# A router's top six experts marked by match-replace: the ranks' transposes and the search of each chunk move to earlier places

## What is computed

```python
logits = x @ gate_w.T
scores = jax.nn.softmax(logits, axis=-1)
topk_w, topk_i = jax.lax.top_k(scores, K)          # K = 6 of E = 64
...
pos = ...   # place of the token among those of its expert, in order of tokens
valid = pos < CAP                                  # CAP = 64
buf = zeros((E, CAP + 1, H)).at[flat_i, slot].set(x[token_ids])
```

```python
proj = hidden_states @ in_proj_w.T;  x, gate = split(proj)
xc = silu(causal_conv(x, 4 taps) + conv_b)
ts, B, C = split(xc @ x_proj_w.T)
```

## Time and profile before

| | us |
|---|---|
| median of 3 runs | 1360.59 (1357.25 to 1361.22) |
| the profiled execution | 1356.37 |
| its span in the trace | 1354.4 |
| stage 1 in it | 264.0 |
| VectorE busy in the span | 1094.3 (81%) |
| TensorE busy in the span | 1277.3 (94%) |
| granted TensorE clock, mean | 0.986 |

### The profile page before, as it was taken

The page is one execution under the profiler, slowest core; times in us unless marked ns, Lnnn a source line. Parts: engine busy times, 40 slices in busy tenths (PEclk is TensorE's granted clock), DMA queues, the critical chain, the costliest instruction groups (busy, mean ns, idle before and its releaser), DMA issues.

```text
span 1354.4 us, 53446 instructions
## 1 busy us (share of the span) xinstructions
PE 1277.3 (94%) x21591; PEld 802.9 (59%) x21591; DVE 1094.3 (81%) x1260; ACT 902.9 (67%) x1920; POOL 878.0 (65%) x522
## 2 busy tenths in 40 slices
PE   6898989599999999999999999999999899999998
PEld 5666767345555545555545555545555578787876
DVE  5798989779999979999889999889999464655554
ACT  4755666478798878888878888778787253434343
POOL 3445348268998978989979899889998330303030
PEclk9999999889999999999999999999999899999999
DMA  8252544859999999999999999999898753122130
GB/s 290 96 229 105 215 153 161 263 166 287 281 308 284 288 273 265 299 298 265 307 260 281 298 265 314 298 262 303 263 309 277 250 201 119 68 80 107 51 134 31
DMA packets 129758, 304.82 MB, mean 225 GB/s; under 512 B 18560, under 2 KB 20352, under 8 KB 127872
## 3 DMA queue, kind: packets, MB, share of 16 engines
q1 hardware_dynamic: 122096, 285.13, 64.3%
q0 software_dynamic: 7600, 18.91, 7.0%
HBM read 213.91 MB, written 56.77 MB: 200 GB/s over the span
## 4 chain that ended last, share of the span: by engine, by line
PE 53%; DVE 10%; issue 9%; POOL 3%; ACT 3%; DMA 1%; DVEq 1%; ACTq 0%; POOLq 0%
PE p_dBx L1337 14%; PE p_dBx L1396 7%; PE p_y L1346 7%; DVE state L1026 7%; PE p_g L1323 6%; PE p_g L1306 4%; PE p_y L1407 2%; PE p_g L1407 2%; PE p_u L1407 2%; PE p_dt L1407 2%; PE p_dt L1286 2%; POOL h_times_C L961 2%; PE p_u L1292 1%; PE p_u L1306 1%; ACT dA L1176 1%
## 5 line engine op out<-in xcount | busy, mean ns | idle before, releaser
L1026 DVE TENSOR_TENSOR_SCAN state<-dA,state_carry,p_dBx 128x512 f32<-128x512 f32 x512 | 626.1, 1266 | 77.0 <-PE p_dBx L1337 74.7
L961 POOL TENSOR_TENSOR h_times_C<-state,C_bcast 128x1024 f32<-128x1024 f32 x128 | 318.0, 2485 | 56.8 <-DVE state L1026 55.9
L961 POOL TENSOR_TENSOR C_bcast<-state,C_bcast 128x1024 f32<-128x1024 f32 x128 | 319.4, 2770 | 23.3 <-DVE state L1026 22.2
L1337 PEld LDWEIGHTS p_dBx<-B_diagonals,step_rows 64*32 64x32 f32 x16384 | 237.1, 106 | 150.4 <-issue 147.6
L1337 PE MATMUL p_dBx<-B_diagonals,step_rows 64*32 64x128 f32 x16384 | 311.2, 276 | 12.6 <-DVE state L1026 7.1
L1176 ACT ACTIVATE dA<-dt_blocks_even,A_par 128x512 f32<-128x512 f32 x256 | 169.6, 710 | 21.5 <-DMA dt_blocks_even<-step_rows 21.5
L1176 ACT ACTIVATE dA<-dt_blocks_odd,A_par 128x512 f32<-128x512 f32 x256 | 169.6, 710 | 20.5 <-DMA dt_blocks_odd<-step_rows 20.5
L280 POOL TENSOR_TENSOR w_in_parts_lo<-C_bcast,w_in_parts_hi 128x512 fp32r<-128x512 f32 x64 | 90.2, 1411 | 107.1 <-ACT w_in_parts_hi L493 106.8
L976 POOL TENSOR_TENSOR step_rows<-step_rows 128x512 f32<-128x512 f32 x16 | 21.9, 1402 | 182.0 <-DMA step_rows<-moe 182.0
L371 DVE SCALAR_TENSOR_TENSOR conv_out<-conv_in,conv_w,conv_out 128x512 f32<-128x512 f32 x96 | 96.1, 1010 | 8.7 <-ACT conv_out L515 6.4
L1306 PE MATMUL p_u<-w_up_pair,step_rows 128*64 128x352 f32 x512 | 92.0, 478 | 3.7 <-issue 2.7
(11 more groups left out here) (186 smaller groups left out, 2114.0 us busy)
## 6 DMA issues: line engine op xcount, KB each, us to landing
w_gate_pair<-in_w_gate SPq DMA_DIRECT2D x32, 1408.0 KB
w_up_pair<-in_w_up SPq DMA_DIRECT2D x32, 1408.0 KB, 7.9
w_down_pair<-in_w_down SPq DMA_DIRECT2D x66, 512.0 KB
dt_blocks_odd<-step_rows SPq DMA_DIRECT2D x256, 64.0 KB
dt_blocks_even<-step_rows SPq DMA_DIRECT2D x240, 64.0 KB
w_down_pair<-in_w_down SPq DMA_DIRECT2D x33, 384.0 KB
g_d<-y_gated SPq DMA_DIRECT2D x33, 256.0 KB, 4.8
sz_d<-silu_gate SPq DMA_DIRECT2D x32, 256.0 KB, 2.1
```

The lines of the kernel that those rows point to most:

```text
L961: pool.tensor_tensor(hc[m][:, b, :, :], hb[:, q, :, :], Cb[:, NM * cp + GS * m:NM * cp + GS * m + GS, :], ALU.mult).then_inc(s_hc, 1)
L1026: ins = dve.tensor_tensor_scan(hb[:, g % NBUF, s, :], dA[:, g % NBUF, s, :], pB[:, g % 2, :].rearrange("p (t s) -> p s t", s=GS)[:, s, :], ...
L1337: ins = pe.matmul(out[DB * p:DB * p + DB, half, j, :, :], dtxT[k, j * P + DB * b:j * P + DB * b + DB], diag[k, ND * cp + 2 * j + p // 2, a ...
```

## The change

`max_index`, the cast, the six comparisons, their sum and the constant `expert_iota` go. In `scores` the last two of the eight largest are overwritten by -1, `match_replace` writes a copy of the scores in which the six largest are -2, and one instruction makes `(copy < 0) * rank`. The ranks' transposes stand in front of tile 8 in every chunk (`RANKS_TURN`; before in front of tile 12 in the last chunk and behind tile 15 in the others), `take_V` behind the first tap of conv 5, and every chunk's search in parts: one behind conv 5, two behind conv 6, one behind conv 7. SP no longer waits for the ranks before it loads the up weights into the place that the comparisons used.

```diff
-        RSTD_AT, RANKS_TURN, X_TURN, SEARCHES, PER_CHUNK = 12, 12, 12, CAP // 16, (T // P) // (NCH - 1)
+        RSTD_AT, RANKS_TURN, X_TURN, SEARCHES, PER_CHUNK = 12, 8, 12, CAP // 16, (T // P) // (NCH - 1)
...
                 if c == NCH - 1:
-                    sp.wait_ge(s_val, NCH)
                     sp.wait_ge(s_spread, 16 * NB * NB)
...
-            pool.iota(eioi[:, :, :], [[0, TJ], [1, E]], base=0, channel_multiplier=0).then_inc(s_const, 1)
...
                 settled()
+                chain(dve.memset(m8[:, :, TOPK:], -1.0))
+                settled()
                 for j in range(TJ):
-                    chain(dve.max_index(ix[:, j, :], m8[:, j, :], xs[:, j, H:XS]))
+                    chain(dve.match_replace(marked[:, j, :], m8[:, j, :], xs[:, j, H:XS], -2.0))
                 settled()
-                chain(dve.tensor_copy(ixf[:, :, :], ix[:, :, :]))
-
-            def ranks(c):
-
-                settled()
-                for k in range(TOPK):
-                    chain(dve.tensor_tensor(eq[:, k, :].rearrange("p (j e) -> p j e", j=TJ), eio[:, :, :],
-                                            ixf[:, :, k:k + 1].to_broadcast([P, TJ, E]), ALU.is_equal))
-                settled()
-                chain(dve.tensor_reduce(chosen[:, :, :].rearrange("p j e -> p (j e)"),
-                                        eq[:, :, :].rearrange("p k n -> p n k"), AX, ALU.add))
-                settled()
-                dve.tensor_tensor(val[:, :, :], chosen[:, :, :],
-                                  tio[:, c * TJ:c * TJ + TJ].unsqueeze(2).to_broadcast([P, TJ, E]), ALU.mult).then_inc(s_val, 1)
+                dve.scalar_tensor_tensor(val[:, :, :], marked[:, :, :], 0.0,
+                                         tio[:, c * TJ:c * TJ + TJ].unsqueeze(2).to_broadcast([P, TJ, E]),
+                                         ALU.is_lt, ALU.mult).then_inc(s_val, 1)
...
             for c in range(NCH):
-                last = c == NCH - 1
-                if c > 0:
-                    for part in range(SEARCHES):
-                        search(c - 1, part)
                 conv(c, 0)
                 softmax_shift(c)
                 conv(c, 1)
                 conv(c, 2)
                 scores(c)
-                if last:
-                    ranks(c)
                 conv(c, 3)
                 conv(c, 4)
-                if not last:
+                if c < NCH - 1:
                     ln_stats(c + 1)
                     ln_norm(c + 1)
                 conv(c, 5)
-                if last:
-                    search(c, 0)
+                search(c, 0)
                 conv(c, 6)
-                if last:
-                    search(c, 1)
-                else:
-                    ranks(c)
+                search(c, 1)
+                search(c, 2)
                 conv(c, 7)
-                if last:
-                    search(c, 2)
-                    search(c, 3)
+                search(c, 3)
```

More of the change, by code:

```diff
@@ L97, in stage1 @@
         m8 = sb("top8", [P, TJ, 8])
-        ix = sb("top8_index", [P, TJ, 8], U32)
-        ixf = sb("top8_index_f", [P, TJ, 8])
-        with ExitStack() as own:
-            eioi = own.enter_context(nc.sbuf_tensor("expert_iota_i", [P, TJ, E], I32))
-        chosen = sb("chosen", [P, TJ, E])
-        eio = sb("expert_iota", [P, TJ, E])
+        marked = sb("chosen_marked", [P, TJ, E])
         tioi = sb("token_rank_i", [P, NCH * TJ], I32)
@@ L107, in stage1 @@
         sio = sb("slot_iota", [E, CAP])
-        eq = tile_in.wu[:, :, :, :].rearrange("p a k i -> p (a k i)")[:, 0:TOPK * TJ * E].rearrange("p (k n) -> p k n", k=TOPK)
         wu_flat = tile_in.wu[:, :, :, :].rearrange("p a k i -> p (a k i)")
-        zl0, r0 = (wu_flat[:, TOPK * TJ * E + n * CH:TOPK * TJ * E + (n + 1) * CH] for n in range(2))
+        zl0, r0 = (wu_flat[:, n * CH:(n + 1) * CH] for n in range(2))
         val = sb("rank_if_chosen", [P, TJ, E])
@@ L327, in _ @@
             dve.memset(V[:, :], 0.0).then_inc(s_dve, 1)
[L328 to L329 removed]
+            dve.wait_ge(s_const, 3)
             dve.tensor_copy(tio[:, :], tioi[:, :]).then_inc(s_dve, 1)
             dve.tensor_copy(sio[:, :], sioi[:, :]).then_inc(s_dve, 1)
[L332 removed]
+            done = [3]
             def chain(ins):
@@ L693, in _ @@
                         turn_x(c + 1)
-                    if n == RANKS_TURN and c == NCH - 1:
+                    if n == RANKS_TURN:
                         turn_ranks(c)
                     in_proj(c, n)
-                if c < NCH - 1:
-                    turn_ranks(c)
                 token_halves(c, wxp, xt, ND, s_xt, s_sps)
```

8 lines of the change are left out of this document (1 added, 7 removed).

## The result

| | us |
|---|---|
| before, median of 10 runs | 1359.87 (1353.58 to 1362.09) |
| after, median of 10 runs | 1368.03 (1364.66 to 1372.05) |
| ratio after to before | 1.0065 [1.0051, 1.008] |
| profiled execution of after, its span | 1372.05, 1370.2 |
| stage 1 in it (before: 264.00) | 276.05 |

The change makes the kernel slower by 8.8 us (6.9 to 10.9). The forecast was 5.8 us more, 1366.4. The two profiles are 15.7 us apart, so they exaggerate: before's profiled execution is among its fastest, after's is the slowest of its ten. The rest of the program behind stage 1, which the change doesn't touch, differs by 3.8 of these (1094.2 against 1090.4). In the other profiles of this study it takes 1089 to 1092. What the change did is to be read in stage 1, and its size from the ratio.

The account below looks back on a forecast made before the run. Stage 1 was taken as bound by SyncE's issues behind gate 3 and, per chunk, the stretch from 1/std to conv 7. Terms 2.9 + 1.4 + 0.3 + 1.2 = 5.8 us on 1360.6 gave 1366.4, range 1361 to 1376.

Parts of the forecast that it names:

- What sets the end: End of stage 1: gate 3 of the last chunk plus about 32 us of SyncE's issues, whatever VectorE does later.
- Rival D: Stage 1's end: not SyncE's; its issues close up and the last chunk's conv 7 decides, 1356.5 us; chance 0.11.
- Term 1: Tail of chunks 0 to 2, normalisation to conv 7's end: 18.62 instead of 17.66 us, +0.96 a chunk, 2.9 in all.
- Term 2: TensorE's four rank transposes, now in front of tile 8, ready without a wait: +0.36 us a chunk, 1.4 in all.
- Term 3: First half of chunks 1 to 3, convs taking turns with GpSimd: 0.3 us for chunks 1 and 2, +1.2 in chunk 3.
- rival E: Convs in tail and chunk 3: turns cost less, GpSimd catches up; +1.9 us, 1362.5, no measurable change; chance 0.21.
- rival C: Seam between chunks: TensorE idles 3.3 us, its clock drops, 2.7 us a chunk, 8 in all, 1374.5; chance 0.08.
- VectorE's idle before normalisation grows to over 10 us: Sign in VectorE's wait for GpSimd's 1/std: idle grows from 3.7 to over 10 us.
- About 3.3 us: Sign at the seam: the last kind of x_proj waits about 3.3 instead of 1.0 us.
- The sum of 5.8: Whole change, all in stage 1: 2.9 + 1.4 + 0.3 + 1.2 us slower.
- the period of 60.8: Sign for the chunks of stage 1: the period becomes about 60.8 instead of 59.4 us.
- granted clock 0.5 behind the seam: Sign on TensorE behind the seam that would show the forecast wrong and the clock's drop (rival C) right.

Follow-up runs that it names:

- the filling: Changed kernel with 6 spare 64x256 matmuls on TensorE in its seam wait in chunks 0 to 2, which kept the clock there: 1362.32 us, ratio 1.0028 to before.
- the order alone: Changed kernel's order, but marked as before by indices and comparisons, ranks right behind the scores: 1384.92 us, ratio 1.0197 to the kernel before.
- The spare matmuls of 64x256: Changed kernel with 12 such matmuls, result unused, on TensorE in the wait for x_proj's last kind, chunks 0 to 2: 1368.88 us, ratio 1.0089 to before.

## Why the prediction was right, and where it was not

- **What sets the end: right.** SyncE's issues behind gate 3 set it in both profiles, and taking VectorE's search away there changed nothing measurable (0.9994). Rival D falls with it. VectorE's lists are done 11.5 us before the stage ends.
- **Term 1, the tail: right in mechanism and nearly in size.** 18.6 us from normalisation to conv 7's end in chunks 0 and 1, as forecast; +0.93 and +0.89. In chunk 2 of the first profile conv 7 took 3.27 instead of 2.74 and it was +1.44, which I can't explain; the second profile's chunk 2 (21.43 from tile 12 to the last kind, against 21.40 in chunk 0) doesn't have it. In sum it is 3.3 against 2.9.
- **Term 2, the transposes: right.** 0.35 against 0.36, no wait.
- **Term 3, the first halves: right, but in the changed kernel's chunk 3 the clock hides it.** Chunks 1 and 2 show 0.54 and 0.55, of which 0.35 are the transposes, so 0.2 each against 0.15. For chunk 3 the forecast was 1.2 and the transposes' 0.36, together 1.56. The changed kernel shows 0.39, which looks like rival E's "GpSimd catches up"; TensorE's waits for low parts up to tile 9 are 0.15, 0.16 and 0.62 us there. With the clock kept it is 1.58. What the forecast couldn't see is that term 3 and rival C overlap: the fall of the clock holds TensorE back at a place where GpSimd sets the pace.
- **Rival C, the clock: given 0.08, and it came at every seam of the changed kernel.** Its price was sized too high but of the right order (8 in all, against some 5.7 in the profile and 5.0 by the filling), its chance badly. The step that failed is what was concluded from the earlier trace rows: that a gap of 2.62 us "is survived", since the four matmuls behind it take 0.65, and so C stays small. Four matmuls right behind a wait are no test. In the second profile of before the four behind the 1.86 us wait also take 0.65, and the clock is at 0.50 one microsecond later; at 254.71 nothing heavy follows that could have shown it. Nor does one wait that is really survived say much of another: of the twelve within the chunks that lasted 2.8 to 3.6 us (six seams of after, three seams and three waits for the ranks in the order alone) the clock fell at nine. What tells them apart, no run shows. The Trainium skill (TensorE: Matmul & The Clock Gate, Why this matters for your kernels) warns of idle gaps between bursts of matmuls; the traces agree at those nine and not at the other three, and here shorter waits were enough too.
- **The total.** The sum of 5.8 lies within the 3.8 (1.2 to 6.3) measured with the clock kept, and mark by mark that profile bears it out: tails +0.91 and +0.89 (and +1.55 in the chunk with the fall in front of tile 12) against 0.96 each, logits to tile 12 +0.51 twice against 0.51, chunk 3 +1.58 against 1.56. (Outside the terms it has +1.5 at the start, where the clock fell once in chunk 0, and -0.5 at the end.) The clock's 5.0 stand on top and make it 8.8. That 1366.4 is all the same only 1.6 us under the median is partly luck. The measured slowdown is 3.0 us more than forecast; the forecast started from a median of three runs that was 0.7 above that of the ten, and the difference of the medians (8.2) is smaller than the ratio gives. More than half of the slowdown is a term that the sum didn't have.
- **The signs.** "VectorE's idle before normalisation grows to over 10 us" was wrong: it is 5.3 to 5.6. The time set free is idle, but it sits earlier, where VectorE waits for ScalarE's taps and TensorE's logits. In chunk 2:

```profile
147.13 2.33 DVE L362 SCALAR_TENSOR_TENSOR conv_out<-conv_in,conv_w,conv_out 128x512 f32<-128x512 f32 x3 [5.23 <-ACT conv_out L486]
151.36 0.43 DVE L369 TENSOR_REDUCE logit_max<-p_small 128x4 f32<-128x256 f32 x1 [1.91 <-PE p_small L633]
156.25 3.45 DVE L362 SCALAR_TENSOR_TENSOR conv_out<-conv_in,conv_w,conv_out 128x512 f32<-128x512 f32 x3 [1.77 <-ACT conv_out L486]
```

  With the 5.30 in front of normalisation that is 14.2 us in this chunk where there were 3.7. "About 3.3 us" for the last kind was right (3.0 to 3.5), the period of 60.8 only without the clock's fall (63.5 and 62.4 with it, between the transposes in front of tile 12), and "granted clock 0.5 behind the seam" was named as the sign of C.

What the forecast did not ask at all is what the marking would be worth with nothing else moved. It priced the 8.6 us of VectorE work a chunk at nothing, since six search steps took their place in the tail. Left empty, that place is worth 8 us.

## What to carry to other kernels

An engine's work that is off the path on average can stand on it for a few microseconds of every round: find the stretch between the last event that another engine gives and the product that another engine waits for, and keep out of it everything that may be done earlier or later. Before a wait of TensorE grows from one to three microseconds, price the clock of the work behind it, and judge whether a gap is survived by a full tile behind it, not by the next few matmuls, and by more than one such gap. Where one engine is held back, look which other engine sets the pace behind it: part of the loss may come back, and hide another. Profile a kernel of this kind twice before a few microseconds between two profiles are explained.

## What the runs showed of the hardware that was not expected

- **The length of a wait alone doesn't tell whether the clock falls.** In front of the last kind it fell behind waits of 1.86, 1.85 and 2.10 us (the kernel before again, and without the last search) and never in the six seams with 1.01. Around 3 us it went both ways: it fell at all six seams of the changed kernel (2.8 to 3.5), but at only one of three in the order alone (3.05, 3.04, 3.05). Behind the 2.62 us of the earlier trace rows it stayed at 1.00 for three microseconds with 1.3 us of work in them. The fall may come in the wait or after it, when the engine is busy again.
- **The clock can also fall where TensorE waits only 1.0 and 0.7 us in quick succession**, at the transposes in front of tile 12: in 7 of the 36 chunks 0 to 2 of the twelve profiles.
- **The clock makes its own next fall.** In the kernel before, a fall in front of tile 12 moved GpSimd against VectorE by about a microsecond, the long instruction came in front of conv 7, and the longer undivided wait was followed by the next fall: in three chunks of three, against none of the six where it hadn't fallen before.
- **Turns between VectorE and GpSimd can make the same instruction take 0.75, 1.65 or 5.10 us**, by which of the two engines was 0.2 to 0.3 us ahead. A profile's duration of such a row contains the wait.
- **The spare matmuls of 64x256 took 0.43 us for each instruction** (12 in 5.1 us), the same form in the x_proj product 0.23 (14 in the 3.24 us of the earlier trace rows, the rows counting two for each instruction). There the instructions alternate between two halves of the output's partitions; the spare ones all wrote the same half. Whether that is the cause wasn't tried.
